# Moving a gated network's last product into the next batch's first slots, and spreading its other products, in a slot-scheduled attention kernel

## The reference, cut to what matters

```python
# x: 16 batches x 512 rows x 256; 16 heads of 16
Q, K, V = proj(Wq, bq), proj(Wk, bk), proj(Wv, bv)
scores = einsum('bhqd,bhkd->bhqk', Q, K) / sqrt(D)
thresh = top_k(scores, 31)[..., -1:]            # the 31st largest of each row
scores = where(scores < thresh, -inf, scores)
context = softmax(scores) @ V
x = layernorm(x + context @ Wo.T + bo)
h = silu(x @ wg.T) * (x @ wu.T)                 # hidden 768; int weights / 127
x = layernorm(x + h @ wd.T)
```

## Time and profile before

| | us |
|---|---|
| median of 3 runs | 2992.36 (2987.83 to 2993.67) |
| profiled execution, its own time | 3002.92 |
| its span | 3001.1 |
| busy share of the span | PE 90%, DVE 83%, ACT 83%, POOL 79% |

### The profile page before, as it was taken

How to read it: one execution, slowest core, us unless ns; L and a number is a source line. 1 busy time by engine, 2 the same in 40 slices (tenths; PEclk the granted TensorE clock), 3 DMA queues, 4 the chain that set the end, 5 groups by cost and what they waited for, 6 DMA issues and landing times.

```text
span 3001.1 us, 81706 instructions
## 1 busy us (share of the span) xinstructions
PE 2705.3 (90%) x21375; PEld 1449.9 (48%) x21375; DVE 2499.2 (83%) x12312; ACT 2478.7 (83%) x5890; POOL 2385.7 (79%) x1668
## 2 busy tenths in 40 slices
PE   5889999989998988899999999999988999899897
PEld 2444544545454444454545455454444545455455
DVE  5888888888889878888898988878888888888883
ACT  4888898888898877888888988878978888888883
POOL 1887888888798876787888888787877879778783
PEclk7899999999999989899999999999999999999998
DMA  3201111020111101111011110211101111110100
GB/s 88 48 21 42 25 41 38 24 49 26 37 30 36 42 21 37 29 29 45 23 42 25 41 39 24 47 27 37 30 25 45 26 40 27 32 42 23 37 2 22
DMA packets 91162, 102.67 MB, mean 34 GB/s; under 512 B 34529, under 2 KB 52962, under 8 KB 90594
## 3 DMA queue, kind: packets, MB, share of 16 engines
q1 hardware_dynamic: 89874, 96.35, 13.4%
q10 hardware_dynamic: 720, 0.14, 0.0%
HBM read 20.86 MB, written 8.39 MB: 10 GB/s over the span
## 4 chain that ended last, share of the span: by engine, by line
PE 36%; DVE 18%; SPq 15%; issue 13%; POOL 8%; ACT 6%; DMA 2%; DVEq 1%; ACTq 0%; POOLq 0%
SPq L386 8%; SPq L385 7%; DVE cand L941 7%; POOL mask L1219 6%; PE bench L740 5%; PE Y_ps L664 5%; PE ST_ps L684 4%; PE Y_ps L661 3%; PE ctxT_ps L698 3%; DVE S L934 3%; PE bench L734 3%; PE bench L605 3%; PE Y_ps L662 3%; PE ST_ps L681 3%; ACT junk L492 2%
## 5 line engine op out<-in xcount | busy, mean ns | idle before, releaser
L1219 POOL TENSOR_SCALAR mask<-S,thr,mb 128x512 bf16<-128x512 f32 x1015 | 2098.4, 2080 | 44.1 <-POOL mb L1213 33.5
L941 DVE MAX8 cand<-Y_ps 128x8 f32<-128x128 f32 x4096 | 1072.0, 282 | 7.4 <-issue 6.9
L492 ACT ACTIVATE junk<-S,at_zero,slope 128x512 bf16<-128x512 f32 x1024 | 824.7, 805 | 99.3 <-DVE S L934 99.2
L934 DVE TENSOR_SCALAR_CACHE_REDUCE S<-S_ps,na 128x512 f32<-128x512 f32 x1024 | 755.9, 738 | 170.7 <-PE S_ps L651 153.2
L502 ACT ACTIVATE above<-S,s,steep 128x512 bf16<-128x512 f32 x1024 | 824.6, 805 | 0.6
L510 ACT ACTIVATE PT<-ST_ps 128x512 f32<-128x512 f32 x1024 | 595.9, 582 | 193.0 <-PE ST_ps L684 187.4
L661 PE MATMUL Y_ps<-ones_b,nbig 128*128 128x512 bf16 x1024 | 403.0, 394 | 169.6 <-DVE cand L941 155.9
L651 PE MATMUL S_ps<-KS,QS 64*128 64x512 f32 x1024 | 523.0, 511 | 4.5 <-DVE S L934 2.3
L664 PE MATMUL Y_ps<-KS,QS 64*128 64x512 f32 x1024 | 523.0, 511 | 0.0
L684 PEld LDWEIGHTS ST_ps<-nbig,mask 128*128 128x128 bf16 x4096 | 235.8, 99 | 382.0 <-issue 382.0
L684 PE MATMUL ST_ps<-nbig,mask 128*128 128x128 bf16 x4096 | 414.8, 225 | 0.0
(11 more groups left out here) (187 smaller groups left out, 3684.6 us busy)
## 6 DMA issues: line engine op xcount, KB each, us to landing
QS<-Qhi SPq DMA_DIRECT2D x512, 32.0 KB, 2.0
KS<-Khi SPq DMA_DIRECT2D x512, 32.0 KB, 2.0
KS<-Klo SPq DMA_DIRECT2D x512, 32.0 KB, 2.0
QS<-Qlo SPq DMA_DIRECT2D x512, 32.0 KB, 2.0
xTs<-in_xT SPq DMA_DIRECT2D x17, 512.0 KB, 3.7
xs<-in_x SPq DMA_DIRECT2D x16, 512.0 KB, 3.9
out<-xs SPq DMA_DIRECT2D x15, 512.0 KB, 2.9
hT<-in_wgT SPq DMA_DIRECT2D x1, 768.0 KB
```

Of the source, the lines that this page charges most:

```text
L492: nc.scalar.activation(junk[:, :], S[:, score_place(j)[0], :], ACT.Tanh, bias=at_zero[:, :], scale=slope[:, hb, col:col + 1], accum_out=s0 ...
L934: nc.vector.tensor_scalar(S[:, at, :], S_ps[n % 2][:, :], na[:, hb, col:col + 1], None, ALU.add, op1=ALU.max, accum_out=rmax[:, n % RING:n ...
L941: mx = nc.vector.max(cand[:, j % CANDS, i, :], Y_ps[j % 2][:, i * BW:(i + 1) * BW])
L1219: nc.gpsimd.tensor_scalar(mask[:, h % MASKS, t, :], S[:, score_place(j)[0], :], thr[:, r:r + 1], mb[:, r:r + 1], ALU.is_lt, op1=ALU.add).t ...
```

## The change

The four `down` leave slots 59 to 62 for slots 1, 2, 3 and 5 of the next batch's pass. What hangs on them follows: the second `layer_norm` from slot 63 to slot 7, the `OUT_SLOTS` from 1 and 2 to 10 and 12. The six pairs of `gate` and `up` now stand in slots 43 to 62, and `gram`, `quad` and `sums` of the second half in 42, 45 and 54. Since batch 1 has no network of a batch before it to finish, `slots(1)` is written ahead of the loops on every engine, and the loops start at batch 2: PE, ACT and POOL with 7 batches in a body, DVE with 2.

```diff
 HALF_USES = {4: "v", 11: "q", 13: "k", 15: "keys", 17: "gram", 19: "quad", 21: "sums",
-             26: "v", 31: "q", 33: "k", 35: "keys", 36: "gram", 37: "quad", 55: "sums"}
+             26: "v", 31: "q", 33: "k", 35: "keys", 42: "gram", 45: "quad", 54: "sums"}
...
-GATE_SLOTS = {42: 0, 44: 1, 46: 2, 49: 3, 51: 4, 53: 5}
-UP_SLOTS = {43: 0, 45: 1, 47: 2, 50: 3, 52: 4, 54: 5}
-DOWN_SLOTS = {59: 0, 60: 1, 61: 2, 62: 3}
+GATE_SLOTS = {43: 0, 46: 1, 49: 2, 52: 3, 58: 4, 61: 5}
+UP_SLOTS = {44: 0, 47: 1, 50: 2, 53: 3, 59: 4, 62: 5}
+DOWN_SLOTS = {1: 0, 2: 1, 3: 2, 5: 3}
...
-LN_SLOTS = {34: 0, 63: 1}
+LN1_SLOT, LN2_SLOT = 34, 7
...
-OUT_SLOTS = {1: (0, 1), 2: (2, 3)}
+OUT_SLOTS = {10: (0, 1), 12: (2, 3)}
...
-        if n in DOWN_SLOTS:
-            uses.append(("down", DOWN_SLOTS[n]))
+    if finish and n in DOWN_SLOTS:
+        uses.append(("down", DOWN_SLOTS[n]))
...
-TURN_OF, ACT_TURN_OF = 5, 7
+TURN_OF, DVE_TURN_OF = 7, 2
...
                     if what == "down":
-                        pe.wait_ge(h_done, b * NF)
+                        pe.wait_ge(h_done, (b - 1) * NF)
                         mm = narrow(part)
...
-            with pe.Fori(1, B, TURN_OF) as b:
+            slots(1, False, False, False)
+            with pe.Fori(2, B, TURN_OF) as b:
                 for i in range(TURN_OF):
-                    slots(b + i, False, False)
-            slots(B, False, True)
+                    slots(b + i, False, False, True)
+            slots(B, False, True, True)
...
                         if what == "down":
-                            row_statistics(b, 1, (part,), taken, use + 1)
+                            row_statistics(b - 1, 1, (part,), taken, use + 1)
...
-            with dve.Fori(1, B, TURN_OF) as b:
-                for i in range(TURN_OF):
-                    slots(b + i, False, False)
-            slots(B, False, True)
+            slots(1, False, False, False)
+            with dve.Fori(2, B, DVE_TURN_OF) as b:
+                for i in range(DVE_TURN_OF):
+                    slots(b + i, False, False, True)
+            slots(B, False, True, True)
...
-                    if not first and not rest and n in LN_SLOTS:
-                        layer_norm(b, LN_SLOTS[n])
+                    if not first and not rest and n == LN1_SLOT:
+                        layer_norm(b, 0)
+                    if finish and n == LN2_SLOT:
+                        layer_norm(b - 1, 1)
```

More of the change, by code:

```diff
@@ L144, in count, with place @@
     return have
[L147 to L153, removed]
+FIRST_COUNT = count(True, False, False)
+SECOND_COUNT = count(False, False, False)
+BATCH_COUNT = count(False, False, True)
+def place(b, n, what, part, first, rest, finish):
+    have = count(first, rest, finish, (n, (what, part)))
     if first:
         return have
-    return (b - 1) * BATCH_COUNT + (FIRST_COUNT + have)
+    if not finish:
+        return FIRST_COUNT + have
+    return (b - 2) * BATCH_COUNT + (FIRST_COUNT + SECOND_COUNT + have)
 def build(nc, xT, x, wqT, wkT, wvT, woT, bq, bk, bv, bo, wgT, wuT, wdT, ident_in, blocks_in, heads_in, ranks_in, out):
@@ L520, in slots @@
                     T = b * TILES + n
-                    uses = uses_of(n - 1, first, rest) if n else []
-                    at = {use: place(b, n - 1, *use, first, rest) for use in uses}
+                    uses = uses_of(n - 1, first, rest, finish) if n else []
+                    at = {use: place(b, n - 1, *use, first, rest, finish) for use in uses}
                     if n % 16 == GROUP % 16 and due(GROUP, n, first, rest):
@@ L574, in _ @@
             slots(1, False, False, False)
-            with act.Fori(2, B, ACT_TURN_OF) as b:
-                for i in range(ACT_TURN_OF):
+            with act.Fori(2, B, TURN_OF) as b:
+                for i in range(TURN_OF):
                     slots(b + i, False, False, True)
@@ L742, in narrow, with on_bench @@
                 return mm
-            def on_bench(b, n, first, rest):
-                for what, part in uses_of(n, first, rest):
-                    use = place(b, n, what, part, first, rest)
+            def on_bench(b, n, first, rest, finish):
+                for what, part in uses_of(n, first, rest, finish):
+                    use = place(b, n, what, part, first, rest, finish)
                     pe.wait_ge(taken, use)
@@ L1061, in late_mask, with slots @@
                                         ALU.is_lt, op1=ALU.add).then_inc(mask_late, 1)
-            def slots(b, first, rest):
+            def slots(b, first, rest, finish):
                 dve.drain()
@@ L1114, in slots @@
                             if part == 0:
-                                summed = place(b, n - 1, "sums", 0, first, rest) + 1
+                                summed = place(b, n - 1, "sums", 0, first, rest, finish) + 1
                                 moments(0, (bench, ready, summed), taken, summed)
@@ L1129, in slots @@
                         row_statistics(b, 0, (2 * part, 2 * part + 1), taken,
-                                       place(b, n - 2, "out_proj", part, first, rest) + 1)
+                                       place(b, n - 2, "out_proj", part, first, rest, finish) + 1)
                     if rest and n < MASK and (n - MASK) % 2:
@@ L1248, in slots @@
                         cut(b, T, n, first)
-                    for what, part in uses_of(n - 1, first, rest) if n else []:
+                    for what, part in uses_of(n - 1, first, rest, finish) if n else []:
                         if what == "up":
-                            use = place(b, n - 1, "up", part, first, rest)
+                            use = place(b, n - 1, "up", part, first, rest, finish)
                             pool.wait_ge(taken, use + 1)
```

44 lines of the change are left out of this document (23 added, 21 removed).

## The result

The changed kernel takes 3055.1 us, the median of 4 runs (3047.11 to 3057.61), beside 2992.2 before: a ratio of 1.0208, with a 95% interval of 1.0187 to 1.0230. It is slower by 63 us.

What follows compares the result with a forecast made beforehand. Each stretch of slots was taken to cost about what its fullest engine, PE or ACT, has to do. Placement +37 and loops +31 make +68 on a median of 2992.4: 3060 us, range 3015 to 3100.

Steps and rivals of the forecast that it cites:

- Slots 0 to 5, +9.7: Slots 0 to 5 gain the `down`s' 10.8 us of PE, 1.1 filling idle time: +9.7 a batch, bounds 9.3 to 10.8.
- Slots 42 to 63, -9.6: Slots 42 to 63 lose the `down`s and fall from 65.6 to 56.0 us: -9.6 a batch, bounds -11.5 to -6.5.
- Spreading, 0: Spreading `gate` and `up` over slots 43 to 62 gives nothing of its own.
- Slots 6 to 16, +1.6: Output normalisation adds 2.4 us of ACT to slots 6 to 16: +1.6 a batch, bounds 0 to +3.
- The wait for `hT`, 1.2 in nine batches: PE waits at slot 1's `down` for POOL's last `hT`: 1.2 us in 9 batches, +11 in all, bounds 0 and 3.
- Placement, +37: All moved steps together: +1.7 us a batch times 15, +26, and the `hT` wait's +11, makes +37.
- The loops: Six DVE jumps at 7.5 us, 45, plus 2 for other engines, less 15.9 for old jumps: +31, bounds +15 to +62.
- Free jumps (3029): Rival: jumps back cost next to nothing, leaving the placement's +37 alone: 3029 us; chance 0.10.
- Rows coming late (3108): Rival: transposed rows and slot 31's load start up to 3.4 us later, `q` waits: up to +48, 3108; chance 0.10.
- Engines that drift apart freely (2942): Rival: only the whole batch must balance, -5.4 a batch, -81, with loops +31 makes -50: 2942; chance 0.09.
- No change (2992): Rival: placement gives 1 us a batch, -15, and jumps at their low bound cost +15: 2992; chance 0.09.

Runs made afterwards that it cites:

- the stretch ahead of it mended: The changed kernel with the fifth `gate` and `up` in slots 59 and 60 and 7 batches in DVE's loop body: 3025.1 us, ratio 1.0108.
- the three kernels with a single move on the old placement: The kernel before with the first `down` in slot 57, or in slot 58, or `sums` in slot 48: 3065.4, 3006.4 and 3018.4 us.
- the mended placement: The changed kernel with `gate`/`up` in 59/60, 7 batches in DVE's body, `down`s in 2, 3, 5, 6: 3000.8 us, ratio 1.0041.

## Why the prediction was right, and where it was not

The time was forecast at 3060 and is 3055, and both halves have nearly the forecast size: loops +33 (forecast +31), placement +30 (forecast +37). That slots 0 to 5 fill with PE work and that DVE's jumps cost as much again was right; that both sums come out so near is in part luck, since their terms were off and cancel. By step:

*Slots 0 to 5, +9.7:* measured +9.1 (23.5 against 14.4), below the low bound of 9.3 by 0.2. PE is full there, as argued.

*Slots 42 to 63, -9.6:* this term was mis-sized. It measured -6.1 in batch 5, just outside its bound of -6.5, and -4.9 in batch 4 (65.6 to 60.7) with its slower slots 55 to 58; over the odd batches 3 to 13 it is -5.2 to -7.6. The step summed PE's and ACT's work and left DVE out, because DVE's busy share was lower. But DVE is late, not full: through the bank's handover in slot 58 (1.81 us) and through `cand` (0.94) its lag becomes PE's, and in most batches PE's clock falls after it. Moving the `gate` alone gave 21 us back. The prediction looked in the trace for full engines and missed two things: that the heavy `down`s were cover for DVE, which the kernel with only the `down`s moved shows (a new wait of 1.88), and that slow clock, which it priced behind the jumps only, is paid here too.

*Spreading, 0:* right. Without it the time is 3053.9.

*Slots 6 to 16, +1.6:* wrong in sign; they shrank by 0.8 (26.3 against 27.1). ACT's L515 passes did come in, but ACT worked 16.06 in slots 0 to 5 where it had worked 14.40, since these last longer, and had more done when slot 6 began. Slots 0 to 16 together have 40.9 us of ACT, 41.1 before. PE's heavy slots were cover for ACT, which the step put at 0.8 and which was larger.

*The wait for `hT`, 1.2 in nine batches:* wrong for the change itself, where only batch 2 shows it (0.72). It was right as a mechanism: with the stretch ahead of it mended it appeared, 1.25 in batch 5 and 17.2 in all. POOL's part of the sum was right: from the start of its eight to the end of the last `hT` it took 19.8 us in batch 5 (1075.80 to 1095.58), forecast 19.6. It was PE that came later than estimated, by its slower slots 57 to 59.

*Placement, +37:* in the batches without a jump the sum is +2.9 on the trace (179.9 against 177.0), forecast +1.7 and the `hT` wait of 1.2. It is right by errors that cancel: 3.5 too much was hoped for in slots 42 to 63, and slots 17 to 41 grew by 0.7 that no term had; against these, 2.4 too much was feared at slots 6 to 16, 1.2 at the `hT` wait and 0.6 at slots 0 to 5.

*The loops:* a DVE jump was put at 7.5 and costs 6.75 in the old placement; six make 40.5. The one jump of PE and POOL ahead of batch 9, put at 2 (ACT's stood there before too), doesn't show in the old placement: slots 0 to 5 of batch 9 take 14.5 in the kernel with the loops alone. In the changed kernel they take 24.5, 1.0 more than in batch 5. The removed jumps were put at 15.9, read from one execution; by the medians of the written-out version they are worth 9.1. The 24.2 us of batch 6 in that execution were not typical: with the same loops, slots 0 to 5 of batch 6 take 20.5, 20.4 and 20.5 in the three kernels with a single move on the old placement. 40.5 - 9.1 = 31, where 33 was measured (28 to 40 by its interval); here too the errors cancel, 4.5 and 2 too much feared against 6.8 too much hoped for. Inside the new placement a jump costs 4.8. The prediction expected the opposite there, a slow clock made dearer by slots full of PE work. In batch 4 of the changed kernel DVE's first stall is shorter (2.37 for 3.60), the second of 1.58 is missing, and the granted clock of the stretch is 0.94, not 0.83. That PE's backlog in these slots also lets DVE catch up is likely, but was not tried apart; nor is it known why the stalls are shorter. Six such jumps in the new placement would be 29, so a part of what is booked above as loops and placement depends on which is counted first.

*The rivals.* Free jumps (3029) fell: 33 us of loops were measured. The rule in the Trainium skill, Runtime: NRT & Kernel Launch, section Instruction fetch mechanics, by which a taken branch out of the prefetched window stalls the engine, agrees with every kernel here that adds or removes jumps of DVE; no trace here shows the fetching itself. The 108 ns that the Trainium skill gives in Advanced Engine Details and Errata, section Control Flow Timing, is not what a jump back of DVE costs here (6.75 us). Rows coming late (3108) fell: PE's wait for `xTs` in slot 31 is 1.02 in batch 5 and was 1.01 there before. Engines that drift apart freely (2942) fell: ACT did use slots 0 to 5 to get ahead, but DVE, late in slots 54 to 59 wherever the work was put, held PE close to itself, by the waits for `cand` and the bank. No change (2992) would have needed a placement worth 1 us a batch, and it cost 2.9.

*What stays open.* Why executions of one kernel differ by as much as the two profiled ones do from their medians (8.0 and 10.7), which is all of the difference between the trace's 44 us and the medians' 63. What makes slots 55 to 58 of the first batch of DVE's body 1.7 us slower than those of the second: DVE has short stalls with no releaser away from the jump back too. The 0.52 in the rows above stands in the kernel before as well (0.52 in slot 58 of batch 4), behind the step where DVE reads a flag and branches on it; batch 4 of the changed kernel has a second one of 0.56 ahead of L1038, and no run isolates them. How a jump's price divides into the stall and PE's slower clock. And the mended placement without any jump back was not run.

## What to carry to other kernels

Before moving a heavy step away, ask who uses its time to catch up: a stretch in which one engine is full can be the cover for another that is late, and that other engine's busy share doesn't show it; look for where its result is read and how far ahead of the reader it stands. A product that takes over a shared buffer from one whose reader is slow should stand some slots behind it: here it waited 4.19, 2.01 and 0 us at 0, 1 and 2 slots, and the kernel took 75, 15 and 0 us more. Count with such a wait what the matrix engine's clock does after it: where it fell, that cost more (1.3 us a batch) than the longer wait itself (0.5). When a rewrite changes the loops and the schedule at once, time them apart first: half of this loss was in the loops, and the best kernel of the study, 0.29% faster, keeps the schedule and only writes out the loops.

## What was not expected of the hardware

A jump back of VectorE's loop stops it twice in the old placement, 2.9 to 3.6 us at once and 1.6 to 1.8 us a few instructions later, and cost 6.75 us a time in all; in the changed kernel it stops once, for 2.3 to 2.6 us, and cost 4.8. Writing out 15 batches instead of 5 for three engines cost nothing that can be seen and gained 9 us. PE's granted clock was 0.83 in slots 0 to 5 of a batch in which DVE alone had jumped, and 1.00 in the next one. A wait of 0.85 us ahead of one product was followed by a slot at half clock, and the same wait of 1.81 us by a fall of the clock in most batches and by none in two.
